# Fetching the edges of an item in eight runs of sixteen instead of one row of 128 prepared on the host

## The reference, cut to what matters

```python
def _graph_conv(x, src, dst, out_norm, in_norm, W, b):
    h = x * out_norm[:, None]
    agg = jax.ops.segment_sum(h[src], dst, num_segments=N_NODES)
    agg = agg * in_norm[:, None]
    return agg @ W + b
...
x = _layernorm(x + _L0_gnn_ref(...), axis=-1)     # three graph_conv with elu
x = _layernorm(x + _L1_gnn_ref(...), axis=-1)     # relu(x[src] + edge_attr @ W_edge.T + b_edge), summed by dst, then an MLP
```

## Time and profile before

| | |
|---|---|
| median of 3 runs | 5461.8 us (5460.47 to 5463.75) |
| profiled execution | 5461.8 us, of which the span of instructions is 5460.0 us |
| busy over the span | PE 91%, DVE 79%, POOL 61%, ACT 43% |
| granted TensorE clock, mean | 0.981 of full speed |
| counting stage | first item at 56 us, last turn ends at 1670 us |

### The profile page before, as it was taken

One profiled execution on the slowest core, in us unless ns is written; L12 is line 12 of the kernel. 1 busy time (PEld: TensorE's weight loads), 2 busy tenths in 40 slices (PEclk: granted clock), 3 DMA queues, 4 the chain that ended last, 5 costly groups with the idle time before them and its releaser, 6 DMA issues.

```text
span 5460.0 us, 113644 instructions
## 1 busy us (share of the span) xinstructions
PE 4990.8 (91%) x40606; PEld 3050.2 (56%) x40647; DVE 4291.1 (79%) x14901; ACT 2364.8 (43%) x4248; POOL 3336.4 (61%) x3421
## 2 busy tenths in 40 slices
PE   7999999999978999999999999888888888887887
PEld 5555666666765555555555544455555555554555
DVE  7788998878996555665666622699999999988997
ACT  5888878888831000000001111344444444444444
POOL 5133443434202777777777777777777777777772
PEclk9999999999998999999999999999999999999997
DMA  6433235444315888888998988422222222222221
GB/s 225 183 125 129 113 121 163 146 147 145 137 53 196 288 284 282 267 289 277 276 280 270 290 294 292 148 46 47 47 45 45 44 45 45 44 44 44 46 45 38
DMA packets 451121, 825.36 MB, mean 151 GB/s; under 512 B 180426, under 2 KB 281676, under 8 KB 443852
## 3 DMA queue, kind: packets, MB, share of 16 engines
q1 hardware_dynamic: 330814, 718.16, 38.7%
q0 software_dynamic: 105200, 74.21, 6.7%
q10 hardware_dynamic: 14541, 25.66, 1.6%
HBM read 615.52 MB, written 202.14 MB: 150 GB/s over the span
## 4 chain that ended last, share of the span: by engine, by line
PE 36%; DVE 25%; POOL 11%; issue 7%; ACT 4%; DMA 2%; POOLq 0%; ACTq 0%; SPq 0%; DVEq 0%
PE banks L2568 21%; DVE tmp L1987 7%; POOL sorted_recs L1261 6%; POOL rows_f L1296 5%; DVE onehot L1974 3%; ACT wide L2205 3%; PE banks L2729 2%; PE banks L2480 2%; DVE rows_f L1994 2%; DVE rows_f L1959 2%; DVE rows_f L1966 2%; PE banks L2443 2%; DVE rows_f L1979 1%; DVE rows_f L1633 1%; DVE rows_f L1638 1%
## 5 line engine op out<-in xcount | busy, mean ns | idle before, releaser
L1296 POOL DMA_INDIRECT rows_f<-table,src_key x1465 | 1416.5, 967 | 463.9 <-issue 439.0
L1261 POOL DMA_INDIRECT sorted_recs<-onehot,rows x1280 | 1236.1, 966 | 460.7 <-issue 378.3
L2205 ACT ACTIVATE wide<-banks 128x784 fp8e4<-128x784 f32 x1563 | 1202.4, 824 | 274.0 <-PE banks L2480 271.8
L2568 PE MATMUL banks<-wide,rows_f 128*128 128x512 fp8e4 (+1 forms) x4900 | 1123.9, 376 | 5.4 <-DMA wide<-counts 5.3
L2443 PE MATMUL banks<-wide,onehot 128*128 128x392 fp8e4 x3125 | 788.1, 333 | 0.2 <-ACT wide L2205 0.2
L1987 DVE TENSOR_SCALAR tmp<-iota_win,rows 128x512 f16<-128x512 f16 x2450 | 752.5, 376 | 0.0
L2480 PE MATMUL banks<-rows_f 128*128 128x196 f16 (+2 forms) x4455 | 669.4, 268 | 68.3 <-DVE rows_f L1638 34.8
L2568 PEld LDWEIGHTS banks<-wide,rows_f 128*128 128x128 f16 x4900 | 442.7, 99 | 384.7 <-issue 8.9
L2480 PEld LDWEIGHTS banks<-rows_f 128*128 128x128 f16 x4455 | 439.1, 153 | 303.4 <-ACT wide L2205 206.6
L2729 PE MATMUL banks<-tmp,rows_f 128*128 128x512 f16 x2450 | 591.8, 382 | 14.6 <-DVE rows_f L1994 14.6
L1164 POOL DMA_INDIRECT onehot<-item_edges_at_dram,rows_f x53 | 60.0, 1132 | 860.9 <-DVE onehot L1404 772.6
(11 more groups left out here) (383 smaller groups left out, 8282.9 us busy)
## 6 DMA issues: line engine op xcount, KB each, us to landing
wide<-counts SPq DMA_DIRECT2D x504, 896.0 KB, 6.6
counts<-wide SPq DMA_DIRECT2D x49, 3136.0 KB
rows_f<-table,src_key POOLq DMA_INDIRECT x1465
sorted_recs<-rows SPq DMA_DIRECT2D x34, 640.0 KB
sorted_recs<-onehot,rows POOLq DMA_INDIRECT x1280
rows_f<-sorted_recs SPq DMA_DIRECT2D x193, 72.0 KB
agg_a<-attr_dram ACTq DMA_DIRECT2D x50, 250.0 KB
agg_b<-attr_dram ACTq DMA_DIRECT2D x50, 250.0 KB
```

The source lines that it names most:

```text
L1261: G.indirect_dma_start(out=sorted_recs[:, :], out_offset=bass.IndirectOffsetOnAxis(ap=keys_of(t, t + 1).bitcast(I32), axis=0), in_=taken[g ...
L1296: G.indirect_dma_start(out=g_rows[:, n % ROW_RING, k, :], out_offset=None, in_=table32[:, :], in_offset=bass.IndirectOffsetOnAxis(ap=src_k ...
L2205: A.activation(win_counts[o.half % 2][:, :, d0:d0 + o.quads * QUAD].rearrange("p b (q c) -> p b q c", c=QUAD), counted, ACT.Copy, scale=UN ...
L2568: last = M(acc_d[m % 2].rearrange("p (h d) -> p h d", h=2)[:, 0:h, :], layer_rows[n][:, block, :], pieces[:, PLACE[k], 0:h, c * HALF:(c + ...
```

## The change

`RUN` becomes 16, so a chunk's items are made of eight runs of 16 edges. The array that the host prepares shrinks to one row per run (16 sources and 16 destinations), and each run of an item is fetched by its own indirect DMA.

```diff
-RUN = 4
+RUN = 16
 RUNS = EDGES // RUN
 RUNS_PER_ITEM = P // RUN
...
+            G.iota(iota_run[:, :], [[1, RUNS_PER_ITEM]], base=0, channel_multiplier=0, **exact)
...
-                G.indirect_dma_start(out=stage[:, c % STAGES, :, :].rearrange("p h e -> p (h e)"), out_offset=None, in_=item_edges_at[:, :],
-                                     in_offset=bass.IndirectOffsetOnAxis(ap=run_idx[:, c:c + 1], axis=0)).then_inc(s_stage[c % STAGES], 16)
+                for j in range(RUNS_PER_ITEM):
+                    G.indirect_dma_start(out=stage[:, c % STAGES, j, :], out_offset=None, in_=edge_runs[:, :],
+                                         in_offset=bass.IndirectOffsetOnAxis(ap=run_idx[:, c, j:j + 1], axis=0)).then_inc(s_stage[c % STAGES], 16)
...
-                V.tensor_scalar(run_idx[:, a:b], first_col[:, a:b], float(PAD_ROW), None, ALU.min).then_inc(s_find, 1)
+                runs = near[:, c, 0:RUNS_PER_ITEM]
+                link(V.tensor_tensor(runs, over_cells(first_col, a, b, RUNS_PER_ITEM),
+                                     iota_run[:, :].rearrange("p (o j) -> p o j", o=1).to_broadcast([P, b - a, RUNS_PER_ITEM]), ALU.add))
+                V.tensor_scalar(run_idx[:, a:b, :], runs, float(PAD_ROW), None, ALU.min).then_inc(s_find, 1)
...
-                dve.wait_ge(s_stage[c % STAGES], 16 * (c // STAGES + 1))
+                dve.wait_ge(s_stage[c % STAGES], 16 * RUNS_PER_ITEM * (c // STAGES + 1))
...
-                edges_src, edges_dst = stage[:, c % STAGES, 0, :], stage[:, c % STAGES, 1, :]
+                edges_src, edges_dst = stage[:, c % STAGES, :, 0:RUN], stage[:, c % STAGES, :, RUN:2 * RUN]
```

More of the change, by code:

```diff
@@ L462, with gnn_kernel @@
 ROW_RING, REC_RING, ATTR_RING, HOT_RING = 6, 4, 4, 4
-def gnn_kernel(nc, x, src, dst, dst_rows, item_edges_at, edge_recs, attr, w_l0, b_l0, w_edge, b_edge, w1, b1, gamma, beta,
+def gnn_kernel(nc, x, src, dst, dst_rows, edge_runs, edge_recs, attr, w_l0, b_l0, w_edge, b_edge, w1, b1, gamma, beta,
                w2, b2, out):
@@ L560, in gnn_kernel @@
         k_row, k_rest = hid_row[0:1, 0:K_SPLIT], dst_key[0:1, 0:SLOTS - K_SPLIT]
-        under = hid_row[:, 4800 + P * LOTS // 2:4800 + P * LOTS // 2 + 15 * FC].rearrange("p (c e) -> p c e", e=FC)
+        under = hid_row[:, SLOTS // 2 + P * LOTS:SLOTS // 2 + P * LOTS + 15 * FC].rearrange("p (c e) -> p c e", e=FC)
         def d0_cells(a, b):
@@ L584, in gnn_kernel @@
         work = onehot_cols(STRIPS * P, 2 * WB * D).rearrange("p (s b f) -> p s b f", s=2, b=WB)
-        stage = onehot_cols(0, STAGES * 2 * P).bitcast(I32).rearrange("p (s h e) -> p s h e", s=STAGES, h=2)
+        stage = onehot_cols(0, STAGES * 2 * P).bitcast(I32).rearrange("p (s r n) -> p s r n", s=STAGES, n=2 * RUN)
         TEMP = STAGES * 2 * P
-        lo_i, hi_i = (onehot_cols(TEMP + n * 2 * P, 2 * P).bitcast(I32).rearrange("p (s e) -> p s e", s=2) for n in range(2))
-        lo_f, key_f = (onehot_cols(TEMP + (2 + n) * 2 * P, 2 * P).rearrange("p (s e) -> p s e", s=2) for n in range(2))
+        lo_i, hi_i = (onehot_cols(TEMP + n * 2 * P, 2 * P).bitcast(I32).rearrange("p (s r n) -> p s r n", s=2, n=RUN) for n in range(2))
+        lo_f, key_f = (onehot_cols(TEMP + (2 + n) * 2 * P, 2 * P).rearrange("p (s r n) -> p s r n", s=2, n=RUN) for n in range(2))
         lo_f2, key_f2 = (onehot_cols(TEMP + (2 + n) * 2 * P, 2 * P).rearrange("p (s e) -> p s e", s=2) for n in range(2))
@@ L595, in gnn_kernel @@
         shift = spare[0:FOLD, 0:2 * FOLD].bitcast(F32)
-        run_idx = spare[:, RUN_AT:RUN_AT + 2 * CHUNKS].bitcast(I32)
+        run_idx = spare[:, RUN_AT:RUN_AT + 2 * RUNS_PER_ITEM * CHUNKS].bitcast(I32).rearrange("p (c j) -> p c j", j=RUNS_PER_ITEM)
+        iota_run = sb("iota_run", [P, RUNS_PER_ITEM])
         ones_h = sb("ones_h", [P, STRIP], F16)
@@ L637, in gnn_kernel @@
         EARLY_AT += EARLY_BUFFERS * GRAN * RECORD
-        assert EARLY_AT <= PADDED * D
-        early_base = hid_row[0:1, 5830:5830 + QCOLS]
+        early_base = tmp_row[0:1, EARLY_AT:EARLY_AT + QCOLS]
+        assert EARLY_AT + QCOLS <= PADDED * D
         early_change = hid_row[0:1, 0:QCOLS]
@@ L2810 @@
     from concourse.bass_utils import run_bass_kernel_spmd
-    ends = [np.pad(np.asarray(a), (0, P), constant_values=-1) for a in (src, dst)]
-    begins = np.arange(RUNS + 1)[:, None] * RUN + np.arange(P)[None, :]
     laid_out = {
@@ L2818 @@
         "dst_rows": np.asarray(dst).reshape(TILES, P),
-        "item_edges_at": np.concatenate([a[begins] for a in ends], axis=1),
+        "edge_runs": np.pad(np.stack([np.asarray(src).reshape(RUNS, RUN), np.asarray(dst).reshape(RUNS, RUN)], axis=1).reshape(RUNS, 2 * RUN),
+                            ((0, 1), (0, 0)), constant_values=-1),
         "edge_recs": np.concatenate([np.asarray(edge_attr_16), np.asarray(src).view(np.float32).reshape(EDGES, 1),
```

## The result

| | before | after |
|---|---|---|
| median, four runs each | 5462.8 us (5460.5 to 5465.5) | 5518.5 us (5515.8 to 5523.5) |
| ratio | | 1.0102 [1.0087, 1.0118] |
| span of the profiled execution | 5460.0 us | 5515.5 us |
| end of the counting stage | 1670.16 us | 1724.11 us |
| rest of the span | 3789.8 us | 3791.4 us |

A forecast was written before the change was run, and what follows sets the result against it. PE was taken to bound turns 9 to 22 and DVE the turns from 41 on, with limits-step and scan-bound turns between. 5461.8 + 2.2 (turn terms) + 21 (POOL's stall) = 5485 us, range 5455 to 5518.

The forecast's parts named there:

- The step that failed: Sixteen scan turns within turns 18 to 38: four scans cost 1.0 us a turn, so 29.8 us each, 476.8 together.
- that term: Turns 18 to 38, scans, limits and largest-feature steps and load of `x` included: 646.1 us for 674.09, -28.0.
- POOL's stall: Turns 42 to 44: eight fetches a chunk queue with puts on POOL, DVE waits before `unpack`, +21 us.
- the lag brought along from chunk 39: POOL's lateness at the opening of fetch 40, in turn 39, assumed as 9.5 us in counting the stall.
- Turns 9 to 17: Counting stage, width 4 to width 2: nine turns at 28.80 us, 259.2 for 255.98, +3.2.
- The start: First chunk's seven extra fetches, covered by 5 us of other DVE work; turns 0 to 8 stay.
- Turn 46: 256 items go from width 1 to width 2 at 0.1856 us each, 47.5 for 33.79, +13.7.
- POOL keeping up (1): POOL's DMAs cost 1.5 us or less each, so no stall: 5464 us, chance 0.16.
- being the bound in width 2 (4): POOL at 2.06 us a DMA uses up the ring in width 2; width 1 stalls about 80: 5544, chance 0.07.
- The scans' waits (3): Scan loads at octet 7 land behind the store, waits stay: +14 to +28, 5499 to 5513 us, chance 0.15.
- Four scans absorbed by ACT's slack (2): Scan turns: four scans cost nothing, a further -16: 5448 us, or 5469 if POOL lags; chance 0.11.
- The extra items (5): Turns 46 to 48: extra items cost nothing and the fetches hide, 5444 us, chance 0.01.

## Why the prediction was wrong

The direction was right and so was the largest mechanism; one saving was sized wrongly, and three small costs were left out.

- **The step that failed: "A turn now has four scans, and six cost turn 33 30.24 - 28.8 = 1.4 us, so four cost 1.0: 29.8 us, 476.8 together".** The sixteen turns take 31.2 us where they are plain, 22 us over 476.8. I took the price of a scan from turn 33 as if it held at any octet, a mean over six. Three of those six, at octets 0, 6 and 12, fall where ACT then waits for PE and cost nothing; the other three cost 0.55 us each. All four places of the changed kernel are paid, at 0.56 us (36.1 us for 64), and the run of the kernel before with hooks at octets 7, 15, 23 and 31 shows 0.54 with no other part of the change. So fewer scans in a turn cost more than six did. About 2 of the 22 us are another thing: a plain turn of the new plan takes 28.94 us, not 28.80. I also laid the length of turns 25 and 26 to the scans, which begin only in turn 27.
- The rest of that term held: ACT's waits went from 28.0 to 1.2 us, the limits step took 35.06 + 39.77 = 74.83 us for 74.8, the largest-feature step cost 5.0 for 5.6, the load of `x` 1.2 for 2.5.
- **POOL's stall: +21 forecast, 18.9 measured**, in turn 44 and at chunk 46 as counted, and the run with later puts took just this away. The mechanism was right, and so was nearly the price, 1.81 us for 1.77. That the size came out so near is in part luck: the dearer DMAs add some 4 us to the lateness, and the lag brought along from chunk 39, put at 9.5 us, was 2.4 (fetch 40 starts at 1260.58 us, and the unpacking that frees its buffer ends at 1258.2).
- Turns 9 to 17: +6.0 for +3.2. Most of the turns run at 28.8 to 29.0 us, and turn 12, in which DVE has 5.8 us of a `find_runs` step, takes 30.3. I had priced only what was new in that step, not that DVE no longer has room for it in width 2.
- The start: +3.8 for nothing. I asked only whether the fetches were in time, not what six more chunks add to the last search ahead of the first transposes.
- Turn 46: +16.5 for +13.7. 256 items take 50.26 us, DVE busy 50.19, so 0.196 us each and not turn 47's 0.186. Turns 39 to 42: +10.6 for +8.6 (three at 38.3, not 37.7). Turn 47 was right, and turn 48's 14 items cost nothing, though DVE fills it.
- The rivals. POOL keeping up (1) and being the bound in width 2 (4) are both out: it is late in one place. The scans' waits (3) didn't stay. Four scans absorbed by ACT's slack (2) is out: ACT's total has room, but the scan hits it where it has none. The extra items (5) were not free, but for those of turn 48.

What stays open: the plan and the fetches apart on a chip of 5,460 us outside the turns named, why a plain turn of the new plan takes 28.94 us, and why other chips run the same program in 7,250.

## What to carry to other kernels

Price a small operation threaded through a loop from the place where it will stand, since an engine with 4 us of slack in a stretch can have none at that point. Look for the waits: just ahead of one a scan was free, just behind one it cost 0.56 us. Better, move it to stretches bound by another engine, which was worth 49 us here, the waits for its loads included. When one transfer becomes eight, count the queue that issues them in the densest stretch and see what stands between them in it: moving the other transfers took away the whole stall. And look for the slack that a slower part lends to the rest, since shortening it can turn the saving into a wait elsewhere.

## What the runs showed of the hardware

- In this trace an indirect DMA of 128 rows holds POOL 0.95 us while DVE stands still and 1.72 us beside DVE operations with two inputs in on-chip memory, in step with DVE's pairs of 2.02 us. The mean over 98 of them in width 1 was 1.81 us with the gap of 0.30.
- A DVE operation of 0.17 us (128x15) took 3.34 us beside two POOL iotas of 0.49 and 2.50 us, and ended 0.1 us after them. With these iotas moved it took 0.17 again.
- A scan of 0.8 us on ACT cost the turn nothing ahead of a wait for PE and 0.56 us where ACT's evictions stood back to back.
- The same program takes 5,463 us on some chips and 7,255 to 7,430 us on others. The change costs 1% on the first. On the second it was timed only with edits: 2.2 to 2.5% with all the remedies of this study, while its plan with one wide fetch costs nothing there that could be told.
